# Four stages of a two-layer model on one core: other banks, routing in smaller pieces, and gathers of expert results in three stages instead of two

## The reference

```python
x = _layernorm(x + _L0_attn_ref(x, ...))   # gate * state-space convolution
x = _layernorm(x + _L0_ffn_ref(x, ...))    # latent attention, then top 2 of 7 experts, computed densely
x = _layernorm(x + _L1_attn_ref(x, ...))   # causal attention, 16 heads of 8
x = _layernorm(x + _L1_ffn_ref(x, ...))    # top 2 of 8 experts, hidden 512, gelu
```

```python
gate_probs = jax.nn.softmax(x @ Wg + bg, axis=-1)
_, top_idx = jax.lax.top_k(gate_probs, 2)
selected = selected / (selected.sum(-1, keepdims=True) + 1e-08)
h = jax.nn.gelu(jnp.einsum('bsf,efh->bseh', x, W1) + b1)
return jnp.einsum('bsef,bse->bsf', jnp.einsum('bseh,ehf->bsef', h, W2) + b2[None, None], selected)
```

## Time and profile before

| | us |
|---|---|
| median of 3 runs (lowest, highest) | 2990.09 (2985.49, 3009.49) |
| profiled execution, its own time | 2997.93 |
| its span, first to last instruction | 2996.2 |
| busy: TensorE, VectorE, ScalarE, GpSimd | 2434.0, 2138.5, 1401.4, 1353.7 |
| convolution, up to its last copy | 133.4 to 209.9 |
| second attention | 1686 to 2540 |
| last stage | 2540 to 2996.2 |
| mean granted TensorE clock | 0.919 |

### The profile page before, as it was taken

One profiled execution on the slowest core, in us unless ns is written; L12 is line 12 of the kernel. 1 busy time (PEld: TensorE's weight loads), 2 busy tenths in 40 slices (PEclk: granted clock), 3 DMA queues, 4 the chain that ended last, 5 costly groups with the idle time before them and its releaser, 6 DMA issues. The chain is left out here.

```text
span 2996.2 us, 49088 instructions
## 1 busy us (share of the span) xinstructions
PE 2434.0 (81%) x15226; PEld 1719.8 (57%) x15226; DVE 2138.5 (71%) x8304; ACT 1401.4 (47%) x2539; POOL 1353.7 (45%) x2639
## 2 busy tenths in 40 slices
PE   4568857999999999488888589999999996799860
PEld 3326745666666665266766456665666653688650
DVE  6537746787877877388888467677787773677773
ACT  3103313666666666122222146556666554688640
POOL 4520023555555554223332135567776655400576
PEclk9979977999999999699999779899999998899985
DMA  3260012322323222423340122222231310677752
GB/s 50 85 217 25 22 14 31 48 43 36 52 34 45 46 33 33 146 74 121 135 169 31 19 36 40 38 45 49 42 55 35 54 35 10 226 251 244 227 157 62
DMA packets 183599, 233.49 MB, mean 78 GB/s; under 512 B 41103, under 2 KB 134256, under 8 KB 175920
## 3 DMA queue, kind: packets, MB, share of 16 engines
q1 hardware_dynamic: 169284, 208.26, 28.5%
q0 software_dynamic: 8192, 16.79, 1.9%
q10 hardware_dynamic: 5868, 5.31, 0.8%
HBM read 138.35 MB, written 70.98 MB: 70 GB/s over the span
## 5 line engine op out<-in xcount | busy, mean ns | idle before, releaser
L1655 PE MATMUL banks<-Kb,Qb 96*128 96x512 f32 (+3 forms) x2048 | 630.1, 355 | 76.0 <-issue 37.0
L1664 PE MATMUL banks<-Qb,Kb 98*128 98x512 f32 (+1 forms) x1408 | 579.2, 416 | 26.4 <-ACT mha_prob L1550 16.3
L1219 DVE CUSTOM_DVE_ANT_0 mha_junk<-banks,mha_mask 128x512 bf16<-128x512 f32 (+3 forms) x1024 | 456.0, 487 | 164.1 <-PE banks L1655 148.8
L1655 PEld LDWEIGHTS banks<-Kb,Qb 96*128 96x128 f32 x2048 | 378.4, 198 | 333.3 <-issue 109.6
L1219 DVE CUSTOM_DVE_ANT_0 mla_junk<-banks,mla_mask 128x512 bf16<-128x512 f32 (+3 forms) x1024 | 453.7, 488 | 158.3 <-PE banks L1655 139.7
L1550 ACT ACTIVATE mha_prob<-banks 128x512 f32<-128x512 f32 (+1 forms) x704 | 375.6, 559 | 295.8 <-PE banks L1664 290.8
L1550 ACT ACTIVATE mla_prob<-banks 128x512 f32<-128x512 f32 (+1 forms) x704 | 374.6, 559 | 270.3 <-PE banks L1664 269.0
L1433 POOL TENSOR_SCALAR_AFFINE_SELECT mla_prob<-mla_prob 128x128 f32<-128x128 f32 (+2 forms) x704 | 235.1, 344 | 289.8 <-PEq L1663 280.9
L1433 POOL TENSOR_SCALAR_AFFINE_SELECT mha_prob<-mha_prob 128x128 f32<-128x128 f32 (+2 forms) x704 | 236.2, 345 | 241.1 <-PEq L1663 225.8
L1664 PEld LDWEIGHTS banks<-Qb,Kb 98*128 98x128 f32 x1408 | 273.7, 195 | 110.7 <-issue 93.4
L2523 POOL DMA_INDIRECT moe_gb<-results,moe_back_slot x128 | 130.4, 1019 | 211.8 <-SPq L2298 174.1
(11 more groups left out here) (495 smaller groups left out, 5054.6 us busy)
## 6 DMA issues: line engine op xcount, KB each, us to landing
moe_wt<-expert_rows SPq DMA_DIRECT2D x46, 1028.0 KB, 5.0
slots<-c_zero SPq DMA_DIRECT2D x16, 1920.0 KB, 10.1
conv_tz<-conv_kernel SPq DMA_DIRECT2D x16, 1024.0 KB, 8.9
moe_xg<-slots SPq DMA_DIRECT2D x46, 256.0 KB, 5.1
results<-moe_yt SPq DMA_DIRECT2D x46, 256.0 KB, 2.6
expert_rows<-glu_row SPq DMA_DIRECT2D x8, 1028.0 KB, 5.1
Qb<-mla_qh SPq DMA_DIRECT2D x128, 64.0 KB
Qb<-mha_qh SPq DMA_DIRECT2D x128, 64.0 KB
```

Of the source, the lines that this page charges most:

```text
L1219: last = dve.tensor_tensor_reduce(junk[:, k % 3, at:at + w], ps[:, bank1(k), at:at + w], mask[:, L - w:L], -1.0, BIG, ALU.add, ALU.min, nm ...
L1655: last = pe.matmul(ps[:, bank1(k), at:at + w], Qb[0:MROW, u, g, h, j * P:(j + 1) * P], Kb[0:MROW, u, g, 0:w], start=True, stop=True)
L1664: pe.matmul(ps[:, bank2(g, k), 0:WIDE[k]].rearrange("p (x w) -> p x w", x=heads), Kb[0:MROW + 2, u, grp, kb * P:(kb + 1) * P], Qb[0:MROW + ...
```

## The change

In the convolution TensorE uses four banks; loads and copies wait for TensorE's own count `c_ready` instead of VectorE's; the gate's weights are prepared in three parts at groups 3, 4, 5 and the latent ones at 8, 9, 10, 11. In the attention the six routing steps become fifteen, the counts move from (2, 11) to (3, 6), and the counts of tiles are taken twice, after sequence 5 and after sequence 11, so that the tables have 16 columns (eight experts twice) instead of 8; they are made in three pieces at (0, 7), (0, 9), (0, 11). In the last stage the first 19 tiles hold sequences 0 to 5, the next 12 sequences 6 to 11, and there are three stages of gathers: after tile 18 (combined at tiles 23, 24, 26, 27, 28, 29), after tile 30 (35, 36, 38, 39, 40, 41) and after tile 45 (sequences 12 to 15, after the loop). `back` finds a row for each half and stands at tiles 4 and 5. The loads at the stage's start have another order, and three constants that the attention's tables already hold are not loaded again.

```diff
@@ convolution_stage @@
-        BX = 2
+        CBANKS = 4
+        BX = CBANKS
...
-        GATE_AT, LATENT_AT = 2, (4, 6, 8, 10)
+        BIAS_AT, GATE_AT, LATENT_AT = 2, (3, 4, 5), (8, 9, 10, 11)
...
-                        sp.wait_ge(t_next, c.next(t_next))
+                        sp.wait_ge(c_ready, g - TBUFS + 1)
...
-                    pool.wait_ge(u_next, c.next(u_next))
+                    if g >= 2:
+                        pool.wait_ge(c_ready, g - 1)
...
-                    u = g % 2
+                    u = g % CBANKS
...
-                dve.sem_inc(c_free, 2)
+                dve.sem_inc(c_free, CBANKS)
                 for g in range(ALL):
                     u = g % 2
                     dve.wait_ge(c_ready, c.next(c_ready))
-                    dve.sem_inc(t_next, 1)
-                    dve.sem_inc(u_next, 1)
                     if g >= 2:
                         dve.wait_ge(y_out[u], c.next(y_out[u], 64))
-                    dve.tensor_copy(y[:, u, :], ps[:, u, :]).then_inc(y_ready, 1)
+                    dve.tensor_copy(y[:, u, :], ps[:, g % CBANKS, :]).then_inc(y_ready, 1)
                     dve.drain().then_inc(c_free, 1)
-                    if g == GATE_AT:
-                        gate_weights()
+                    if g in GATE_AT:
+                        gate_weights(GATE_AT.index(g))
@@ attention_stage @@
-        ROUTE = dict(pe=(1, 7), act=(1, 8), logits=(1, 11), dve=((2, 1), (2, 3), (2, 6), (2, 8), (3, 1), (3, 6)),
-                     counts=(2, 11), pool=8, tiles=(0, 6))
+        ROUTE = dict(pe=(1, 7), act=(1, 8), logits=(1, 11), counts=(3, 6), pool=8,
+                     dve=((2, 1), (2, 2), (2, 3), (2, 6), (2, 7), (2, 8), (2, 9), (2, 10), (2, 11), (3, 0), (3, 1), (3, 2),
+                          (3, 8), (3, 9), (3, 11)), tiles=((0, 7), (0, 9), (0, 11)))
...
+                            if not latent and n == SENT + ROUTED_AT and at in ROUTE["tiles"]:
+                                (tiles, tile_places, tile_tables)[ROUTE["tiles"].index(at)]()
...
                     if step == 0:
                         dve.wait_ge(rl_ready, c.next(rl_ready))
                         link(dve.tensor_tensor(lg, ps[:, MB, 0:BLK * E1].rearrange("p (t e) -> p t e", e=E1),
                                                over(D.rb), ALU.add))
                         dve.sem_inc(mb_free, 1)
+                    if step == 1:
                         highest(lg, m1)
-                    if step == 1:
+                    if step == 2:
+                        ranked()
+                    if step == 3:
                         chosen(s1)
                         dve.tensor_tensor(pr, lg, each(m1), ALU.subtract)
+                    if step == 4:
                         link(dve.scalar_tensor_tensor(ex, s1, NEG, lg, ALU.mult, ALU.add))
-                    if step == 2:
+                    if step == 5:
                         highest(ex, m2)
+                    if step == 6:
+                        ranked()
+                    if step == 7:
                         chosen(s2)
-                    if step == 3:
+                        dve.tensor_copy(run[:, 0, :], run[:, BLK, :])
+                    if step == 8:
                         link(dve.tensor_tensor(took[:, :, :], s1, s2, ALU.add))
-                        link(dve.tensor_copy(run[:, 0, :], run[:, BLK, :]))
-                        for b in range(BLK):
-                            link(dve.tensor_tensor(run[:, b + 1, :], run[:, b, :], took[:, b, :], ALU.add))
-                        dve.sem_inc(took_ready, 1)
-                    if step == 4:
+                    if step in (9, 10):
+                        later(2 * step - 18)
+                        later(2 * step - 17)
+                    if step == 11:
+                        dve.drain().then_inc(took_ready, 1)
+                    if step == 12:
                         dve.wait_ge(count_ready, c.next(count_ready))
-                        if r == SENT - 1:
-                            link(dve.tensor_scalar(D.need, ps[:, MB, BLK * E1:(BLK + 1) * E1], 1.0 / L,
+                        if r in (SENT // 2 - 1, SENT - 1):
+                            at = 0 if r < SENT - 1 else E1
+                            link(dve.tensor_scalar(need[:, at:at + E1], ps[:, MB, BLK * E1:(BLK + 1) * E1], 1.0 / L,
                                                    (L - 1.0) / L - 0.499, ALU.mult, ALU.add))
                         link(dve.tensor_tensor(pos, ps[:, MB, 0:BLK * E1].rearrange("p (t e) -> p t e", e=E1),
                                                over(D.cap), ALU.add))
                         dve.sem_inc(mb_free, 1)
-                        place(0, s1)
...
                 def tiles():
-                    t = nt
...
+                    dve.wait_ge(tile_consts, 3 * 16)
+                    link(dve.tensor_scalar(need[:, :], need[:, :], MAGIC, None, ALU.add))
+                    link(dve.tensor_scalar(need[:, :], need[:, :], -MAGIC, None, ALU.add))
+                    link(dve.tensor_tensor(need[:, E1:S], need[:, E1:S], need[:, 0:E1], ALU.subtract))
+                    link(dve.tensor_tensor(part, low, need[:, :].unsqueeze(1).broadcast_to([P, S, S]), ALU.mult))
+                    link(dve.tensor_reduce(D.base, part, axis=AX.X, op=ALU.add))
+
+                def tile_places():
+                    link(dve.tensor_tensor(past, steps, D.base[0:1, :].unsqueeze(1).broadcast_to([1, nt, S]), ALU.is_ge))
+                    dve.tensor_copy(to[:, 0:1], place0[:, 0:1])
+                    link(dve.tensor_tensor(to[:, 1:S + 1], place0[:, 1:S + 1], D.base[0:1, :], ALU.subtract))
+                    link(dve.tensor_tensor(to[:, E1:S], to[:, E1:S], need[0:1, 0:E1], ALU.add))
+                    link(dve.tensor_tensor(delta, to[:, 1:S + 1], to[:, 0:S], ALU.subtract))
...
+
+                def tile_tables():
+                    link(dve.tensor_tensor(past, past, delta.unsqueeze(1).broadcast_to([1, nt, S]), ALU.mult))
                     link(dve.tensor_reduce(before, past, axis=AX.X, op=ALU.add))
@@ gelu_experts_stage @@
-        COUNT, PLACE, GATES, MOVE = 1, (0, 2), ((2, 1), (3, 1)), (4, 1)
+        COUNT, PLACE, GATES, MOVE = 1, (0, 2), ((2, 1), (3, 1)), ((4, 1), (5, 1))
...
+        HALF = SENT + SPARE
+        STAGES = ((HALF, range(0, SENT // 2)), (TILES[0], range(SENT // 2, SENT)), (ALL, range(SENT, NB)))
         COMBINE, LATE = {}, []
-        for q, (_, n) in enumerate(GROUPS):
-            for j in range(n):
-                g = FIRST[q + 1] + 4 + (5 * j + 2) // 4 if q + 1 < len(GROUPS) else ALL
+        for after, seqs in STAGES:
+            for j, s in enumerate(seqs):
+                g = after + 4 + (5 * j + 2) // 4 if after < ALL else ALL
+                q = int(s >= SENT)
                 if g < ALL:
-                    COMBINE[g] = (q, j)
+                    COMBINE[g] = (q, s - GROUPS[q][0])
                 else:
-                    LATE.append((q, j))
+                    LATE.append((q, s - GROUPS[q][0]))
...
-                sp.dma_start(wr[:, :], io["Wg"]).then_inc(consts, 16)
-                sp.dma_start(rb[:, :], rows(io["bg"])).then_inc(consts, 16)
-                sp.dma_start(tri[:, :], io["c_tri"]).then_inc(consts, 16)
-                sp.dma_start(low[:, :, :], rows(io["c_low"])).then_inc(consts, 16)
-                sp.dma_start(steps[:, :, :], io["c_steps"][:, 0:TILES[1], :]).then_inc(consts, 16)
                 c = Counts(sp)
+
+                def constants():
+                    sp.dma_start(tri[:, :], io["c_tri"]).then_inc(consts, 16)
+                    sp.dma_start(low[:, :, :], rows(io["c_low"][0:E1, 0:E1])).then_inc(consts, 16)
+                    sp.dma_start(steps[:, :, :], io["c_steps"][:, 0:TILES[1], 0:E1]).then_inc(consts, 16)
...
-                    if group_of(g)[1] == TILES[group_of(g)[0]] - 1:
+                    if g + 1 in [after for after, _ in STAGES]:
...
-                for g in range(WBUFS):
+                load_w(0)
+                load_x(0)
+                constants()
+                for g in range(1, XBUFS):
                     load_w(g)
-                for g in range(XBUFS + 1):
                     load_x(g)
+                for g in range(XBUFS, WBUFS):
+                    load_w(g)
+                load_x(XBUFS)
...
+                    dve.wait_ge(consts, 3 * 16)
+                    link(dve.tensor_copy(trib[:, :], tri[:, :]))
...
-                def back():
-                    n = SENT * BLK
...
+                def back(a):
+                    n, half = SENT * BLK, SENT * BLK // 2
+                    sel = (D.sel1, D.sel2)[a]
+
+                    def of(vector, out, lo, hi):
+                        w = hi - lo
+                        link(dve.tensor_tensor(eq[:, 0:w, :], sel[:, lo:hi, :], vector.unsqueeze(1).broadcast_to([P, w, E1]),
+                                               ALU.mult))
```

(28 more changed lines are left out.)

123 lines of the change are left out of this document (64 added, 59 removed).

## The result

| | before | changed |
|---|---|---|
| median of 20 runs, us | 2996.55 | 2978.96 |
| lowest, highest | 2984.76, 3010.29 | 2970.52, 2989.91 |
| profiled execution: time, span | 2997.93, 2996.2 | 2977.37, 2975.6 |

The ratio of the changed kernel to the kernel before is 0.9939, with an interval of 0.9922 to 0.9957: 18 us faster, where 33 us were forecast (2957 against 2990.09). With 20 runs the median of the kernel before came out 6.5 us above that of the three shown ahead, so against it the forecast was 40 us: the direction was right and the size twice too large. The time lies in the stated range, near its upper end (2982). The two profiled executions differ by 20.6 us, where the sum said 39.

The account below looks back on a forecast made before the run. Bounds: y stores in convolution, TensorE in attention, constants and queued tokens, TensorE, then GpSimd's gathers in the last stage. Terms summed to -39 on 2997.93, giving 2959, median put at 2957; range 2936 to 2982.

Parts of the forecast that it names:

- The last step, from 2959 to 2957: Whole kernel: moves the sum to the median run, since that run is 7.8 us faster than the profiled one.
- Routing in fifteen pieces, -14: Second attention: TensorE's three waits for VectorE's maxima nearly vanish, 1.2 us in each of 12 sequences; ends 0 and 17.
- Rival (a): Attention: TensorE's time is not the bound, VectorE's gain is waited for at ScalarE, clock falls as before; 2972, chance 0.27.
- Clock, -11: Second attention: half of the 22.4 us lost to falls of TensorE's clock goes with the waits; ends 0 and 22.
- The rival in which the clock stays up: Attention: all 22 us of clock loss and the 3.4 us wait go; 2945, chance 0.22.
- Tile tables, 0: Attention: tables grow from 3.7 to about 6.5 us, but waits sum to about the same; ends +3 and -3.
- Start of the last stage, -11: No waiting for constants, first tile's loads first; first product at about 2554.1 instead of 2565.09; ends -6 and -12.
- `back`, +4: Last stage, tiles 4 and 5: two halves take VectorE 10.05 us, less 3.9 before and 1.9 free; ends 2 and 6.
- gathers, -5: Last stage: three stages of gathers let GpSimd begin the last four sequences earlier, gain 4.7 us; ends +4 and -33.
- Convolution, -2: Convolution: four banks and earlier weight loads let the last few copies see faster stores; ends +3 and -8.
- still 3.5: Convolution: sign of being right, VectorE's copies from PSUM still 3.5 us apart.
- The rival that ends slower: Last stage: six waits for gathers each leave a tile at half clock, 39 us lost; 2996, chance 0.04.

Follow-up runs that it names:

- d_load_g3: Changed kernel plus nine unused VectorE operations (1.9 us) per routed sequence behind units (3,3), (3,4), (3,5); attention's first to thirteenth copy 592.3 us.
- n_route_early: Changed kernel with the last three routing steps at (3,7), (3,8), (3,9), counts at (3,5), running counts done by (3,1); ratio 0.9909 to the kernel before.
- u_conv2: Changed kernel with the old convolution stage (two banks, loads counted by VectorE); the convolution's last copies began at 211.46 us.
- n_defer: Changed kernel, gather combinations two tiles apart, last routing steps earlier, a stage's last root after the next stage's first gathers, sequence 11 combined after the loop; ratio 0.9839.
- u_start: Changed kernel with the old order of loads and waits for constants at the last stage's start; 33.3 us from last copy to first product.
- n_back_late: Changed kernel with the two halves of back at tiles 7 and 11 instead of 4 and 5; 149.1 us from first product to tile 18's store.
- n_warm: Changed kernel with 110 unused TensorE transposes at the attention's end; 25.4 us from last copy to first product.

## Why the prediction was wrong in size

The parts of the sum gave -39 and the two profiled executions differ by 20.6 us. Of the 18 us between them 8 are the routing with its clock, 3 the start of the last stage, 1.5 the tile tables, and 4 a stretch that the forecast put at nothing and that varies by 10 us between profiles. The other parts were off by less than 1 us each. The last step, from 2959 to 2957, took the median run to be 7.8 us faster than the profiled one, from three runs; with twenty the difference is 1.4.

**Routing in fifteen pieces, -14: the step that failed.** It was 0.6 us a sequence, 7 us in all, not 1.2. The three waits of 1.44 us did go. The step took the removed waits for the gain, because "the rest falls among units of 256 columns, where it has time to spare". There was no time to spare: `d_load_g3` and `n_route_early` show that work anywhere from (2,1) on delays the sequence, and about half of the removed waits came back at its end, before the low half and the next scores. The trace of the kernel before held the answer: VectorE's timeline has no pause above 0.27 us in the 27 us around the routing steps. The view of TensorE's waits, on which the step went, names where TensorE waits, not where VectorE's backlog began. Rival (a) had this loss at the wrong engine; the waits for ScalarE stayed at 16.3 as in the earlier trace rows.

**Clock, -11: right in size, in part by luck.** 18 us from first to thirteenth copy, less 7 for the waits, leave 11. But "half" was a choice between two ends, and kernels with the same pieces took anything from 564.3 to 578.3 us for this stretch, as the clock fell in it or not. The rival in which the clock stays up was wrong for the changed kernel's profile, whose distances still hold one of 49.9 and one of 49.8; from the first to the thirteenth copy it came true in `u_conv2`, `n_route_early` and `n_defer` (granted 1.00). The prediction cites the Trainium skill, "TensorE: Matmul & The Clock Gate", section "A second HAM failure mode: psum-queue depth-cycling", for small pauses between groups of matmuls that make the clock swing; the runs agree in part only. With the three waits gone the granted clock rose from 0.97 to 0.99. But `d_load_g3`, with more waits than the kernel before had, was granted 0.99 too. Which pauses make the clock fall is open.

**Tile tables, 0: too low.** One wait of 3.41 us became three that sum to 5.4, not to about the same. From the thirteenth to the fourteenth copy it is 52.7 us instead of 50.4; the fifteen profiles of kernels with the new tables give 52.0 to 54.7, so +3 is nearer, the upper of its ends.

**Start of the last stage, -11: -8.** The order of loads did what was said (7.2 by `u_start`). The 3 us are the logits, which the step took over at 3.72 us from an execution in which the clock had risen in their midst. The lower end, a constant that lands late, stood behind it and was hidden by the slow logits.

**`back`, +4; gathers, -5: right**, at +4.9 and -4.6. The stall of 29.5 us was 30.5, the rest behind the last store 53.9 was 53.7. For `back` the size alone is right: `n_back_late` shows that setting 1.9 us of idle time per tile against it, as the step did, doesn't hold. What the forecast passed over is that the stall of the gathers was set by a choice of six tile numbers a stage, and worth 29 us.

**Convolution, -2: right in size by luck.** It was -1.4 in the two profiles and -2.5 between the means, but as the difference of two parts that the step didn't have: copies 2.98 us apart, where "still 3.5" was named as the sign of being right, and a third copy 7.2 us later. The faster pace was in its far end only ("all copies after the first three at the 3 us that an early landing allows"), and the later start in none.

The rival that ends slower (each new wait leaves a tile at half clock) did not come: the stall is 30.5 us, no more than the 32.85 before.

## What to carry to other kernels

Before work is moved into "light" places, find where the engine that does it has last been idle, and where it is idle next: work moved within that stretch still costs, and cutting it into pieces gives back less than the waits that vanish (here 0.6 of 1.44 us a sequence, and what the clock adds). An average spare time per tile is not to be set against one long piece, either. Where a queue serves at a pace of its own (12.3 us a sequence here), ask for its results at that pace; a further stage of the pipeline is worth little until this is so (4 us here, and 41 after). And a row that holds several instructions (x2) is not one step: count them before a gap is called a stall.

## What was not expected of the hardware

The same 32 products took 3.7 to 4.1 us in seven profiles and 6.8 us in nine, after 16 to 23 us of rest in all but one of them, as TensorE's clock rose at about their start or not. The one, `n_warm`, rested for 4.09 us behind 12.17 us of transposes at clock 1.00, and the clock still fell to 0.50 within the next 2.6 us of work. A duration read from one execution close to such a rest holds for either level, and should enter a sum with both.
